# Fused attention and feed-forward kernel: where the third maxima unit of an attention step stands

## The reference, cut to what matters

```python
# x: (16, 1024, 256), float32; 16 heads of width 8
left = x_normed[..., :128]
q, k, v = (left @ W.T).reshape(N, S, 16, 8)       # for Wq, Wk, Wv
energy = jnp.einsum('nqhd,nkhd->nqkh', q, k)
att = jax.nn.softmax(energy / 4.0, axis=2)
out = jnp.einsum('nqkh,nkhd->nqhd', att, v) @ Wo.T + bo
x = x + layernorm(out)
# feed-forward on layernorm(x): three cycles of a four-layer gated net, then
x = x + layernorm(ffn(layernorm(x)))
```

## Time and profile before

| | |
|---|---|
| median of 3 runs | 3422.21 us (3420.38 to 3422.49) |
| the profiled execution: span from first to last instruction | 3418.2 us |
| busy share of the span | PE 96%, DVE 87%, ACT 85%, POOL 29% |
| mean granted TensorE clock, whole span | 0.986 |
| one attention stage (that of batch 7) | some 128 us |
| the 30 beats behind it | some 77 us |

### The profile page before, as it was taken

One profiled execution on the slowest core, in us unless ns is written; L12 is line 12 of the kernel. 1 busy time (PEld: TensorE's weight loads), 2 busy tenths in 40 slices (PEclk: granted clock), 3 DMA queues, 4 the chain that ended last, 5 costly groups with the idle time before them and its releaser, 6 DMA issues.

```text
span 3418.2 us, 55797 instructions
## 1 busy us (share of the span) xinstructions
PE 3280.1 (96%) x19328; PEld 931.1 (27%) x19328; DVE 2961.0 (87%) x5517; ACT 2896.0 (85%) x3806; POOL 976.6 (29%) x1382
## 2 busy tenths in 40 slices
PE   6989999999999999999999999999999999999987
PEld 2222232322323232232322323232232322323222
DVE  7999989888898988989888898988989888898942
ACT  3868979798897979889798897979989798896975
POOL 5012060421506033060421406033060421505024
PEclk7998999999999999999999999999999999999999
DMA  3111111121112111111121111111121121111001
GB/s 89 26 41 43 37 44 32 43 49 43 51 33 54 39 49 43 43 50 32 43 50 43 51 33 50 41 46 47 36 57 33 43 49 44 38 32 50 7 22 37
DMA packets 97337, 144.71 MB, mean 42 GB/s; under 512 B 49312, under 2 KB 59936, under 8 KB 89248
## 3 DMA queue, kind: packets, MB, share of 16 engines
q1 hardware_dynamic: 93360, 123.83, 13.7%
q0 software_dynamic: 3696, 17.31, 2.7%
HBM read 34.61 MB, written 32.51 MB: 20 GB/s over the span
## 4 chain that ended last, share of the span: by engine, by line
PE 69%; DVE 14%; ACT 8%; issue 4%; SPq 2%; POOL 2%; DMA 1%; DVEq 0%; POOLq 0%
PE heads_ps L503 24%; PE ring_ps L470 15%; PE scoresT_ps L488 11%; DVE max_parts L949 10%; PE scoresT_ps L590 7%; ACT p_sb L700 4%; PE scoresT_ps L595 3%; DVE stats L960 2%; PE scoresT_ps L598 2%; ACT headsT L709 1%; PE scoresT_ps L601 1%; PE ring_ps L532 1%; SPq L337 1%; PE scoresT_ps L518 1%; PE heads_ps L470 1%
## 5 line engine op out<-in xcount | busy, mean ns | idle before, releaser
L949 DVE TENSOR_REDUCE max_parts<-ring_ps 128x1 f32<-128x512 f32 x3741 | 2365.5, 682 | 230.0 <-PE ring_ps L470 171.1
L700 ACT ACTIVATE p_sb<-scoresT_ps 128x1024 f32<-128x1024 f32 x2048 | 1970.2, 1025 | 84.6 <-PE scoresT_ps L488 60.8
L470 PE MATMUL ring_ps<-k_rows,q_rows 48*128 48x512 bf16 x3741 | 1078.0, 385 | 23.5 <-DVE max_parts L949 14.4
L503 PE MATMUL heads_ps<-p_sb,v_sb 128*9 128x512 f32 x8192 | 1073.3, 596 | 17.9 <-ACT headsT L709 11.9
L488 PE MATMUL scoresT_ps<-q_rows,k_rows 51*128 51x512 bf16 x4096 | 1021.8, 384 | 15.0 <-ACT p_sb L700 7.5
L470 PEld LDWEIGHTS ring_ps<-k_rows,q_rows 48*128 48x128 bf16 x3741 | 263.5, 94 | 1319.9 <-DVE max_parts L949 1209.6
L1210 POOL CAST max_wide<-max_all 128x16 bf16<-128x16 f32 x128 | 25.1, 196 | 1753.7 <-DVE max_all L955 1753.7
L590 PE MATMUL scoresT_ps<-state,w 128*128 128x512 f32 x736 | 365.4, 619 | 5.9 <-DVE state L1013 3.9
L488 PEld LDWEIGHTS scoresT_ps<-q_rows,k_rows 51*128 51x128 bf16 x4096 | 207.7, 94 | 243.7 <-ACT p_sb L700 219.9
L811 ACT ACTIVATE p_sb<-scoresT_ps,b 128x512 f32<-128x512 f32 x180 | 123.5, 686 | 165.6 <-PE scoresT_ps L590 164.6
L503 PEld LDWEIGHTS heads_ps<-p_sb,v_sb 128*9 128x9 f32 x8192 | 124.7, 89 | 289.6 <-issue 278.6
(11 more groups left out here) (206 smaller groups left out, 2757.7 us busy)
## 6 DMA issues: line engine op xcount, KB each, us to landing
q_rows<-parts SPq DMA_DIRECT2D x744, 32.0 KB
k_rows<-parts SPq DMA_DIRECT2D x744, 32.0 KB
x_sb<-in_x SPq DMA_DIRECT2D x16, 1024.0 KB, 4.9
x_in<-in_x SPq DMA_DIRECT2D x15, 1024.0 KB, 5.1
out<-x_sb SPq DMA_DIRECT2D x15, 1024.0 KB, 3.9
out<-x_in POOLq DMA_DIRECT2D x15, 1024.0 KB, 7.8
q_rows<-max_rows SPq DMA_DIRECT2D x512, 3.0 KB
feat_h<-headsT SPq DMA_DIRECT2D x512, 16.0 KB
```

The costliest lines, as they stand in the source:

```text
L470: e.matmul(ring_bank(max_taken, u + 1), q_rows[rows, slot, pair, h * BANK + qb * P:h * BANK + (qb + 1) * P], k_rows[rows, slot, pair, kh * ...
L503: m = e.matmul(heads_ps[32 * j:32 * j + DH + 1, :], v_sb[:, b % 2, kb, 4 * (group % NG) + j, 0:DH + 1], p_sb[:, n % 2, j, :], start=(kb == ...
L700: e.activation(p_sb[:, n % 2, 2 * two:2 * two + 2, :].rearrange("p h n -> p (h n)"), scoresT_ps[:, 2 * two * BANK:(2 * two + 2) * BANK], A ...
L949: e.tensor_reduce(max_parts[:, gi % 2, kh, col:col + 1], bank_of(max_taken, u + 1), AX.X, ALU.max).then_inc(max_taken, 1)
```

## The change

```diff
             if b == 0:
                 return units_until(LEAD0 + 4 * n + (1, 3, 4)[third])
-            return units_until(b * UNITS + LEAD + min(IN_ATTENTION, 3 * n + (2, 2, 3)[third]))
+            return units_until(b * UNITS + LEAD + min(IN_ATTENTION, 3 * n + (3, 3, 3)[third]))
```

## The result

The changed kernel takes 3465.7 us (median of four runs, 3464.8 to 3471.3) against 3421.3 us before: a ratio of 1.0132, 95% interval 1.0118 to 1.0147. It is 44 us slower, where the prediction had +36. Runs in a rare slow state are left out of every time here: beside the first four experiments the kernel before took 4038 and 6442 us in two of its 14 runs. The profiled execution has a span of 3463.0 us, 44.8 more than that of before.

The account below looks back on a forecast made before the run. Before, a PE-ACT circle of 1.985 us a step was the bound; after, a bank circle of 2.055. Fourteen stages at +2.45 (+34) and batch 15 at +2.1 gave +36, so 3458 us, range 3440 to 3476.

Parts of the forecast that it names:

- The bound before: Ordinary attention steps of the old order: a circle through PE and ACT sets the step, 1.985 us, PE's work 1.95.
- PE's own 1.95: PE's matmul work in an ordinary attention step, 1.95 us, claimed to stay the same after the change.
- ACT's circle: Old order's loop from weighing through exponentials to the second pair two steps on: 3.97 us for two steps, 1.985 each.
- What the change takes away: Between weighing and next exponential: the unit leaves that path, one slot of 0.22 to 0.24 us goes from ACT's wait.
- The circle over the bank: Third unit waits for the bank DVE empties last, delaying second pair and weighing: 4.11 us for two steps, 2.055 each.
- Copies hidden: Copies of heads, one per eight steps, cost nothing extra thanks to ACT's lead of 0.075 us: 16.44 us per eight steps.
- Stage by stage: Each of fourteen attention stages: +2.4 us in steps 3 to 63, +0.28 at the beginning, -0.2 at the end, +2.45 together.
- The last batch: Batch 15, with 48 steps that have units: +2.1 us.
- The clock: Rival: granted clock falls to 1.2 GHz in one step in fifty, +35 us on top, 3493 us; chance 1%.
- a rival of 1%: The case of a fall to 1.2 GHz while PE idles between groups for PSUM banks: 3493 us, chance 1%.
- the sentence that batch 0 speaks against a fall: Batch 0: a unit holds PE in each step (0.21 idle), yet granted clock is 0.99, nearly throughout 2.4 GHz.

Follow-up runs that it names:

- the first four experiments: Changed order with 480-column reductions, 256-column reductions in changed and old order, third unit between second pair and weighing: 3408.7, 3345.4, 3382.6, 3427.2 us.
- Experiment 2: Changed kernel with each reduction of the maxima over 256 of 512 columns, half the maximum left out: 3345.4 us, ratio 0.9777.
- experiment 3: Kernel before, in its old order, with each reduction over 256 of 512 columns, half the maximum left out: 3382.6 us, ratio 0.9886.
- experiment 7: Changed kernel, except that in step 0 the third unit stands behind the second pair, as before: 3463.7 us, ratio 1.0125.
- Experiment 4: Changed kernel with the third unit moved to between the second pair and the weighing: 3427.2 us, ratio 1.0012.

## Why the prediction was right, point by point

- **The bound before** (PE's own 1.95, ACT's circle 1.985): right. Experiment 2 reaches 1.95 where neither ACT's slot nor a bank is in the way; experiment 3 keeps 3.96 for two steps with reductions more than a third shorter (0.42 against 0.68).
- **What the change takes away**: right. An exponential starts 0.45 behind its first pair (1558.90 to 1559.35), against 0.68 before, which the prediction counted from the unit ahead of that pair.

```profile
1559.35 3.89 ACT L700 ACTIVATE p_sb<-scoresT_ps 128x1024 f32<-128x1024 f32 x4 [0.16 <-PE scoresT_ps L488]
```

- **The circle over the bank**, 4.11 us for two steps: 4.10. Shown, not only argued: its length followed the reduction's length (4.00 at 480 columns) until PE's 3.90 took over (256 columns), and moving the one unit behind the second pair removed it.
- **Copies hidden**: right. Around the copy at 1554.93 the first pairs stand at 1554.80 and 1556.74, 1.94 apart, an ordinary short step.

```profile
1554.93 0.60 ACT L709 ACTIVATE headsT<-heads_ps 128x512 f32<-128x512 f32 x1
```
```profile
1554.80 0.39 PE L488 MATMUL scoresT_ps<-q_rows,k_rows 51*128 51x512 bf16 x2
...
1556.74 0.39 PE L488 MATMUL scoresT_ps<-q_rows,k_rows 51*128 51x512 bf16 x2
```

- **Stage by stage**: +2.4 for steps 3 to 63, +0.28 for the first steps and -0.2 behind them were 2.45, 0.27 and -0.21 in the trace of batch 7: 2.5 us a stage, 35 us for fourteen. The last batch was +1.6 instead of +2.1.
- **The clock** is the term that was mis-sized: it stood at nothing in the sum and as a rival of 1% whose place was the ordinary steps. The trace has it at the beginnings of stages: six stages with a fall, 1.6 to 2.0 us longer than their neighbours, and 1.8 more at batch 1, less the 1.6 that batch 11 had before, 10 us in all. With the 35 and 1.6 this is 47. What lies between and behind the attention stages gives 2 back: two stages of beats were 1.0 longer before (those behind batches 9 and 10), the one behind batch 14 is 1.6 longer now, and what is behind batch 15 is 1.2 shorter. So 45 is what the spans differ by. The step that failed was the sentence that batch 0 speaks against a fall. It spoke for the short holds of ordinary steps, and there it was right. It said nothing about the beginning of a stage, where PE stands for the bank in step 0 and step 1 and for ACT between them, 0.77 us of 3.40 (busy 2.63 in the first window above). Batch 0 itself has a fall there, which the mean of 0.99 over its 158 us hides; a window of the kernel before, 2.8 us behind that stage's first exponential:

```profile
77.60:81.00 3.40, 3.40 (x20) 0.66 (x16) 2.53 (x5) 1.94 (x4) 0.00 (x0) 0.51 0.13 29
```

Why the changed kernel has six such falls in the stages of batches 2 to 14 and the kernel before one stays open (table below experiment 7), so the term is known in its size, 10 us, and not in its cause. The Trainium skill (TensorE: Matmul & The Clock Gate, Part 1, the section on psum-queue depth-cycling) says that brief idle times between groups of matmuls, where banks are cycled, can let the clock go down and up again. In the attention stages the trace has such falls at their beginnings alone, in six of the 14 of batches 2 to 15, at 1.6 us for most, and it does not show that idle time brings them; it has none in the ordinary steps, which hold PE for 0.2 us in every second step at full clock.

No version here beats the kernel before with whole reductions. Experiment 4 comes within 0.12% of it.

## What to carry to other kernels

A ring of buffers has a latency circle of its own, fill, wait for the consumer, consume in order, free, and it can bind where the consumer's busy time does not: here DVE needs 1.81 us of a 2.05 us step, and the circle through it still sets the pace. Its length is a sum of start-to-start distances that a trace of the old order already has. Before a producer is moved ahead of critical work in a queue that keeps its order, add up start-to-start distances around the circle that its buffer closes, and compare the sum with the circle that the move shortens. And look at the first steps of a stage apart from the steady ones, in a window short enough that a mean does not hide them: here the holds of the first steps cost 0.27 us a stage, some 4 us in all, and more falls of the clock at those places, of which the cause stayed open, cost 10.

## What the runs showed of the hardware

- One fall of the granted clock to 1.2 GHz for 3.4 us costs 1.6 us at these stage beginnings. PE had stood 0.77 of the 3.40 us ahead of it; stages beside it, with the same instructions and the same 0.77, had no fall, and experiment 3, with 0.88 idle there, had none in 13 of 14 stages.
- A circle of 4.10 us over two steps is not shared evenly: steps alternate between 1.95 and 2.15 for a while, then drift to 2.00 and 2.10 behind a join, with the same sum.
- A reduction of 512 columns takes 0.68 us, of 480 columns 0.65 and of 256 columns 0.42; so 0.033 us for 32 columns, as the circle's change by 0.10 for three of them confirms.
